# A four-block transformer on one core: the order of work comes from another dispatcher, which places every engine's pieces one by one

## What is computed

```python
x = _L0_xcond_ref(x, cond, ctx, ...)   # full self attention with a mask, RoPE; cross attention; tanh-gelu MLP
x = _L1_xcond_ref(...)                 # full self attention; cross attention; tanh-gelu MLP
x = _L2_xcond_ref(...)                 # self attention in windows of 128; top-16 cross attention; swiglu MLP
x = _L3_xcond_ref(...)                 # full self attention, RoPE; cross attention with RoPE; erf-gelu MLP
# each block, in outline:
h = layernorm(x) * (1 + scale) + shift
q, k, v = split(h @ w_qkv + b)
x = x + gate * (softmax(q @ k.T / 4) @ v) @ w_o
x = x + gate * cross_attention(layernorm(x), ctx)
x = x + gate * (act(layernorm(x) @ w_1) @ w_2)
```

## Time and profile before

| | us |
|---|---|
| median of 3 runs | 3004.18 (3001.68 to 3004.83) |
| span of the profiled execution | 3001.3 |
| TensorE (PE) busy in it | 2791.8, 93% |
| VectorE (DVE) busy | 2002.4, 67% |
| ScalarE (ACT) busy | 1400.1, 47% |
| GpSimd (POOL) busy | 638.6, 21% |
| mean granted TensorE clock | 0.978 |

### The profile page before, as it was taken

The page is one execution under the profiler, slowest core; times in us unless marked ns, Lnnn a source line. Parts: engine busy times, 40 slices in busy tenths (PEclk is TensorE's granted clock), DMA queues, the critical chain, the costliest instruction groups (busy, mean ns, idle before and its releaser), DMA issues.

```text
span 3001.3 us, 48815 instructions
## 1 busy us (share of the span) xinstructions
PE 2791.8 (93%) x15447; PEld 1384.9 (46%) x15447; DVE 2002.4 (67%) x4848; ACT 1400.1 (47%) x2571; POOL 638.6 (21%) x967
## 2 busy tenths in 40 slices
PE   8999999999999998999988888889799999999899
PEld 5533344335536324334465566666553433333556
DVE  7778387643683865884355669677888694886631
ACT  3255635663453663664635233322225355577341
POOL 2010011221410110131124435424321000112220
PEclk9999999999999999999999999999999999999899
DMA  7323122322551312243166415531232042123521
GB/s 208 103 66 121 47 64 78 107 66 85 155 164 41 92 50 75 68 131 94 40 191 184 132 49 175 155 89 35 94 103 57 15 128 51 44 58 100 180 92 37
DMA packets 268160, 286.87 MB, mean 96 GB/s; under 512 B 70665, under 2 KB 207243, under 8 KB 267275
## 3 DMA queue, kind: packets, MB, share of 16 engines
q1 hardware_dynamic: 256651, 282.28, 32.0%
q0 software_dynamic: 11264, 1.46, 0.3%
HBM read 167.43 MB, written 114.72 MB: 94 GB/s over the span
## 4 chain that ended last, share of the span: by engine, by line
PE 68%; DVE 13%; issue 7%; DMA 5%; POOL 2%; ACT 2%; SPq 2%; DVEq 0%; ACTq 0%; POOLq 0%
PE ring_c L1491 11%; PE ring_b L1458 11%; PE ring_a L1414 10%; PE ring_a L1526 7%; PE ring_b L1514 6%; PE ring_b L1457 4%; PE ring_a L1503 3%; PE ring_b L1371 3%; DVE row_max L1776 2%; PE ring_a L1514 1%; DMA reciprocals<-scr_recip 1%; PE ring_a L1386 1%; DMA q_ring<-neg_max_parts 1%; PE ring_b L1485 1%; PE ring_b L1336 1%
## 5 line engine op out<-in xcount | busy, mean ns | idle before, releaser
L1599 ACT ACTIVATE probs<-ring_b 128x512 f32<-128x512 f32 (+1 forms) x1728 | 904.8, 604 | 498.0 <-PE ring_b L1458 434.8
L1776 DVE TENSOR_REDUCE row_max<-ring_a 128x1 f32<-128x1024 f32 x512 | 600.1, 1219 | 130.5 <-PE ring_a L1414 127.6
L1458 PE MATMUL ring_b<-q_ring,k_ring 100*128 100x512 bf16 x1536 | 514.0, 381 | 20.9 <-ACT probs L1599 4.8
L1414 PE MATMUL ring_a<-k_ring,q_ring 96*128 96x512 bf16 x1536 | 450.8, 383 | 21.0 <-issue 3.8
L1491 PE MATMUL ring_c<-probs,v_and_ones 128*17 128x512 f32 x3072 | 400.9, 599 | 5.3 <-ACT probs L1599 4.8
L1882 POOL CAST neg_max_parts<-neg_max 16x128 bf16<-16x128 f32 x112 | 33.0, 294 | 1594.7 <-ACT neg_max L1593 1265.6
L1773 DVE CUSTOM_DVE_ANT_0 w_mlp<-ring_a,w_mlp 128x1024 bf16<-128x1024 f32 x256 | 300.6, 1221 | 53.2 <-PE ring_a L1414 52.6
L1820 DVE TENSOR_TENSOR x_tok<-x_tok,ring_a 128x512 f32<-128x512 f32 x96 | 66.0, 688 | 338.8 <-PE ring_a L1526 206.7
L1458 PEld LDWEIGHTS ring_b<-q_ring,k_ring 100*128 100x128 bf16 x1536 | 142.2, 97 | 313.3 <-issue 210.1
L1414 PEld LDWEIGHTS ring_a<-k_ring,q_ring 96*128 96x128 bf16 x1536 | 127.6, 98 | 298.8 <-issue 219.9
L1514 PE MATMUL ring_b<-h_feat,w_mlp 128*128 128x512 f32 x512 | 229.9, 597 | 3.6 <-ACT h_feat L1570 1.7
(11 more groups left out here) (149 smaller groups left out, 3726.7 us busy)
## 6 DMA issues: line engine op xcount, KB each, us to landing
q_ring<-scr_q SPq DMA_DIRECT2D x128, 384.0 KB, 4.4
scr_q<-split SPq DMA_DIRECT2D x64, 384.0 KB, 2.9
k_ring<-scr_k SPq DMA_DIRECT2D x64, 384.0 KB, 5.2
scr_q<-split SPq DMA_DIRECT2D x64, 256.0 KB, 3.1
scr_out<-out_stage SPq DMA_DIRECT2D x128, 128.0 KB, 2.6
scr_out<-out_stage SPq DMA_DIRECT2D x64, 256.0 KB, 2.2
h_feat<-scr_out SPq DMA_DIRECT2D x56, 256.0 KB
reciprocals<-scr_recip SPq DMA_DIRECT2D x56, 256.0 KB
```

What stands on the lines that cost most here:

```text
L1414: last = mm(ps[:, half * BLOCK:(half + 1) * BLOCK], q[0:PARTS, h, t * P:(t + 1) * P], k_view(g)[0:PARTS, h, half * BLOCK:(half + 1) * BLOC ...
L1458: last = mm(ps[:, :], k_view(g)[0:ROWS, h, s.kt * P:(s.kt + 1) * P], q[0:ROWS, h, q0:q0 + BLOCK], start=not g.masked, stop=True)
L1599: f(PT[0:n, s.pt, :], ps[0:n, :], ACT.Exp, **kw).then_inc(b_evac, 1)
L1776: v.tensor_reduce(NM[:, s.nm, s.u:s.u + 1], ps, AX.X, ALU.max).then_inc(a_evac, 1)
```

## The change

The engines' instructions are the same, each with the same operands: 1123 DMA issues on SP, 4338 instructions on DVE and 971 on POOL in both. TensorE's 11795 matmuls become 11682 by the fillers alone (2071 to 1958), and ScalarE's activation table loads go from 27 to 35. What changes is the order on every engine.

`play` is gone. `run` now dispatches one phase at a time: the first phase of a step whose inputs are ready, or the next phase of a step under way (one queue each for ring a, ring b and the rest). The engine that can start something first gets it, with the lowest rank among all pieces that are ready within the new `REACH`. Each engine's order is what was dispatched to it (`order[eng]`). A slot of a ring is taken when TensorE begins, by `place`. Fillers are placed in the same pass. Rank tables are new, the second batch element starts after `DELAY` 100 instead of 200, and nearly all durations and latencies are fitted anew; a matmul piece is also charged for a switch to or from `pv`.

```diff
-LINK = dict(PE=0.22, ACT=0.16, DVE=0.13, POOL=0.12, SP=0.1)
+LINK = dict(PE=0.31, ACT=0.14, DVE=0.13, POOL=0.1, SP=0.0)
...
+    def issue(self, s, n, at):
+
+        eng, us = s["ph"][n]
+        last = n == len(s["ph"]) - 1
+        if eng == "PE":
+            self.fill(s, at)
+            if s.kind == "pv":
+                us += 0.155 * (self.before != "pv")
+            elif self.before == "pv":
+                us += 0.166 if s.kind in WIDE else 0.075
...
+        self.free[eng] = at + us
+        self.order[eng].append(s)
...
+        if not last:
+            self.queue[s.get("ring") or "c"].append((s, n + 1, end))
+            return
...
     def run(self):
         while True:
...
+            self.pump()
+            ready = []
+            for t in self.threads:
+                if t.want is not None:
+                    at = self.begin(t)
+                    if at is not None:
+                        ready.append((at, t.rank, t.n, t, t.want, 0, t.want["ph"][0][0]))
+            for q in self.queue.values():
+                if q:
+                    s, n, at = q[0]
+                    eng = s["ph"][n][0]
+                    ready.append((max(at, self.free[eng]), s["rank"], 0, None, s, n, eng))
...
+            at, _, _, _, _, _, eng = min(ready, key=lambda x: x[:3])
+            at, rank, _, t, s, n, _ = min((x for x in ready if x[6] == eng and x[0] <= at + REACH[eng]), key=lambda x: x[1:3] + x[:1])
...
-REACH = dict(PE=0.05, ACT=0.25, DVE=1.2, POOL=5, SP=0.1)
...
+REACH = dict(PE=0.0, ACT=0.1, DVE=0.0, POOL=1.2, SP=0.3)
+DELAY = (7.5, 100)
...
-FAR, SLOW, SLACK = 1.15, 1.02, 0.3
...
-    p.pe_order = play(p.steps, None, FAR, SLOW)
-    play(p.steps, p.pe_order, 1.0, 1.0)
...
-            for s in whole.pe_order:
+            for s in whole.order["PE"]:
```

More of the change, by code:

```diff
@@ L1118, in _ @@
             sp.dma_start(COLS[:], ins["cols"]).then_inc(consts_in, 16)
-            for s in steps:
+            for s in whole.order["SP"]:
                 if s.kind == "early_load":
@@ L1551, in _ @@
             act.wait_ge(setup_dve, 1)
-            for s in steps:
+            for s in whole.order["ACT"]:
                 if s.kind == "mask":
@@ L1652, in _ @@
             junk = {}
-            for s in steps:
+            for s in whole.order["DVE"]:
                 if s.kind == "mod":
@@ L1837, in _ @@
             ones2 = float(np.array([0x3F803F80], np.uint32).view(np.float32)[0])
-            for s in steps:
+            for s in whole.order["POOL"]:
                 if s.kind == "k_ones":
```

483 lines of the change are left out of this document (210 added, 273 removed).

## The result

The changed kernel takes 3020.07 us (median of 4 runs, 3014.91 to 3021.68) against 3003.59 us for the kernel before beside it (4 runs): ratio 1.0059, 95% interval 1.0042 to 1.0076. It is **0.6% slower**. The forecast was 2972, 1.1% faster; the time lies outside its range of 2940 to 3016, on the side of the two slower rivals.

What follows compares the result with a forecast made beforehand. TensorE, busy 2791.8 of 3001.3 us, was taken as the bound, with 500.6 us of idle and fillers to win. Terms -15.9 - 10.7 - 5.3 = -31.9 us gave 2972 us, 1.1% faster, range 2940 to 3016 (own range 2955 to 2992).

Steps and rivals of the forecast that it cites:

- the two slower rivals: Thinner work beside the chain to w_out (3028 us, chance 0.16), and a lower mean TensorE clock (3002 us, chance 0.06).
- Where the idle time sits: TensorE idles 209.5 us, 100.5 of it in L2's top-16 attention, in many small waits; chains rather than capacity bound that stretch.
- the two idle terms: Less TensorE idle before second-pass pieces (-10.7 us) and before first-pass pieces (-5.3 us).
- the clock at 0: The sum had no clock term; a lower TensorE clock stood only as a rival, +30 us.
- second-pass term: Runs of second-pass pieces that fill ring b go from 184 to 90: -10.7 us of TensorE's wait, ends 0 and -46.
- first-pass term: Filler groups between first-pass pieces fall from 109 to 81: -5.3 us of TensorE idle, ends 0 and -21.
- Fillers, -15.9: 113 fewer TensorE fillers at 0.141 us each: -15.9 us, or 0 if the waits stay.
- The chain to w_out, 0: Reciprocal-to-multiplication chain nears 16.5 us, but less work stands beside it: 0 for both, between +24 and -24 us.
- The thin cover: Rival: too little TensorE work beside the chain to w_out, so late reads stop TensorE: +24 us, 3028, chance 0.16.
- Table loads, 0: ScalarE loads 35 tables instead of 27, mostly in L2, covered by TensorE's work: 0, other end +10.3 us.
- The clock's rival: Fewer fillers lower TensorE's mean clock by 0.01, +30 us, taking the gain back: 3002 us, chance 0.06.
- More from the top-16 stretch: Rival: closed-up top-16 chains in L2 remove a third of its idle, -33 us more: 2939 us, chance 0.14.

Runs made afterwards that it cites:

- a_late: Changed kernel with TensorE's order from its 2644th piece on remade by the old second pass without allowances: 3000.65 us, ratio 0.9997.
- the kernel without allowances: Changed kernel with TensorE's whole order remade by the old second pass, waits and work counted 1.0 instead of 1.15 and 1.02: 3000.50 us, ratio 0.9993.

## Why the prediction was wrong

| us | forecast | measured |
|---|---|---|
| fillers | -15.9 | -21.7 |
| of idle: before second-pass pieces | -10.7 | +1.6 |
| of idle: before first-pass pieces | -5.3 | +6.3 |
| all idle time | -16.0 | +4.7 |
| real work (the clock) | 0 | +33 |
| span | -31.9 | +16.0 |

*Where the idle time sits.* Right as a reading: waits are small and many. Wrong in what I took from it, that a re-ordering that plans fewer waits has fewer.

*The steps that failed: the two idle terms, and the clock at 0.* The second-pass term (-10.7) and the first-pass term (-5.3) both have the wrong sign. Counting runs of pieces (184 to 90, 109 to 81) said nothing on the pattern that mattered: the pairs of first-pass pieces stand among MLP pieces, and the 7 fillers of a round stand before an MLP piece. The three places of the change that were compared have no such round. Runs of pieces were counted, and not which pieces between those of ring a had gone. In place of the gain the runs showed 15 us lost in these rounds, which TensorE's order of another making (a_late) brings back. And the sum had no term for the clock; the real work grew by 33 us, more than the whole forecast.

*Fillers, -15.9.* Their number was right, and 21.7 us of them did go. Idle rose by only 4.7, so this term came about as forecast; with the idle terms, 17 of 31.9 us arrived. The two runs without fillers do not price it. They take fillers away and leave the waits, which costs 0.027 us per filler in the old order (56/2071) and 0.012 in the new (23/1958); the term is for a filler that goes together with its wait. The far end of the term, 0, was too good as well: a filler that goes while the wait stays is a loss.

*The chain to w_out, 0.* The earlier trace rows were misread: they join steps of different chains. SyncE and VectorE take their steps in the plan's order, so the chains can be told apart. The read issued at 861.00 has its reciprocal at 886.34 (870.98 is that of the read of 846.83), and the multiplication at 1351.63 belongs to a read of 1311.43. The chain of 1342.44 goes on so (timeline 1325:1362):

```profile
1347.82 0.34 DVE L1808 RECIPROCAL denominators<-denominators 128x32 f32<-128x32 f32 x1
1348.19 0.61 SPq L1270 DMA_DIRECT2D scr_recip<-denominators  x1
...
1352.48 0.59 SPq L1279 DMA_DIRECT2D reciprocals<-scr_recip  x1
1356.78 0.69 DVE L1814 TENSOR_TENSOR h_feat<-h_feat,reciprocals 128x512 f32<-128x512 f32 x1 [3.05 <-DMA reciprocals<-scr_recip]
```

It takes 15.0 us from the read's issue, not 9.9. Over all 64 multiplications the shortest such chain of that trace is 9.5 us, so the least chain of 16.5 us holds by luck; the median is 27.6 us before and 18.2 in the changed kernel. So the gain that was named and not priced is there: booked one phase at a time, the chains are shorter. The thin cover came in part too: w_out waits 14.9 us for the multiplication (6.3 before), below the 20 that I had named as its mark, and the 22 us of 700 to 800 lie around it. A stall of 5.00 us there is the collision with GpSimd, which no term had. The rival's time, 3028, was nearer than the forecast's, but its reason (DMA allowances gone) is not what the runs show: in these queues allowances made TensorE's order worse.

*Table loads, 0.* 35 loads of 1283 ns, as said. ScalarE is busy 21.4 us longer, of which they are 10.3; TensorE's wait for exp of the top-16 scores went from 12.5 to 22.1 us. Up to 10 us of the loss may be here; no run took it apart.

*The clock's rival.* Its mark (mean under 0.97) was met, 0.964, and its size was about right: +30 us were named, 33 measured. Its time (3002) missed because the gain that it was to take back was 17 us and not 32: 3004 - 17 + 33 = 3020. It should have been a term of the sum. Its reason, fewer fillers, is not shown: more fillers raised the clock to 0.980 and the time rose too, and the kernel without allowances runs in 3000.50 us at a mean clock of 0.970.

*More from the top-16 stretch.* GpSimd's top-16 steps began 33 us later and ended 20 us earlier (1716.0 to 2217.5), and L2 as a whole did win (1400 to 1700 of real work: -34 us). What came behind them gave it back: VectorE is busy 57.9 and 54.8 of 60 us in 2100:2160 and 2160:2220 (54.1 and 53.4 before), the granted clock is 0.91 and 0.81 there (0.94 and 0.91), and then TensorE runs in pairs.

*The range.* The forecast's own range, 2955 to 2992, does not follow from the ends that it names: -46 for the second-pass term gives 2937, and all terms at 0 give 3004.

What stays open: why 700 to 800 takes 22 us and 1000 to 1100 14 us more. Both stay in every kernel with the new dispatcher's queues (138 to 146 and 145 to 147 us). So they belong to the other engines' orders or to the order within each ring, which the second pass keeps, and not to how the rings are interleaved. Part of the first is the clock: from 850 to 870 us TensorE works without a pause at 1.2 GHz (the row stands in the last section), which costs by the durations there some 9 us (an estimate: 20 us, by 1.05 us against 1.91). The two losses are paid for by the 62 us won elsewhere.

## What to carry to other kernels

A planner's fillers, or its booked waits, are its opinion and not a measure. A run without fillers tells what they are worth while the waits stay; it does not tell what a wait is worth that goes away. Split the difference of two spans into fillers, idle and real work before naming a cause, and compare two orders along the work done, not along the clock. When a scheduler lets each thread ask for one piece at a time, look for rounds in which two pieces of one kind take all slots of a ring while a piece for the other ring stands behind in its thread. And keep GpSimd's SBUF instructions short where VectorE's chain is short of time: cutting two products into four instructions each gave 0.4 to 0.5% to both orders at no other change.

## What the runs showed of the hardware that was not expected

A VectorE instruction with two inputs in SBUF, and some casts and scalings there, wait inside their own duration for a GpSimd instruction under way, up to 4.40 us for 0.69. The same operation with one input in PSUM does not (687 ns median, 690 at most), nor does one that reads a single tensor for statistics (410 and 428). TensorE can be busy without a pause and stay at 1.2 GHz: in the changed kernel it is busy 19.87 of the 20 us from 850 to 870 with a granted clock of 0.50, after 14.9 of the 20 us before, and 33.4 of the 40 us from 860 to 900 with 0.79,

```profile
830.00:845.00 15.00, 11.41 (x90) 4.47 (x90) 4.16 (x7) 10.58 (x21) 7.41 (x17) 1.00 0.85 248
845.00:850.00 5.00, 3.45 (x14) 0.68 (x13) 1.95 (x2) 1.52 (x4) 2.90 (x8) 0.59 0.89 254
850.00:870.00 20.00, 19.87 (x62) 6.36 (x59) 13.40 (x15) 6.83 (x11) 0.47 (x1) 0.50 0.57 149
860.00:900.00 40.00, 33.43 (x146) 19.51 (x145) 25.92 (x46) 7.67 (x12) 10.49 (x10) 0.79 0.50 142
```

where eight cross products take 1.91 us (at 856.16 and 862.38) instead of 1.05. And 2000 fillers, 270 to 290 us of busy TensorE, are worth 23 to 56 us.
